# A gated recurrence over 512 steps: the rows of the input products stored first at a block's edge, and the second half's r and m transposed as they come and summed in two instructions

## The reference

```python
def step(h, x_t):
    fused = sigmoid(concatenate([x_t, h], -1) @ w_W + w_b)
    hidden_state, output_state = split(fused, 2, -1)           # r and z below
    memory_state = x_t @ wx_W + wx_b + hidden_state * (h @ wh_W + wh_b)   # m below
    h_new = output_state * h + (1.0 - output_state) * tanh(memory_state)
    return (h_new, h_new)
_, hs = lax.scan(step, h0, swapaxes(x, 0, 1))
return x + swapaxes(hs, 0, 1)
```

## Time and profile before

| | us |
|---|---|
| median of 3 runs | 1673.91 |
| lowest and highest run | 1670.84, 1674.57 |
| the profiled execution | 1674.5 |
| its span, first to last instruction | 1672.7 |
| busy: PE / PEld | 1627.8 / 1343.3 |
| busy: DVE / ACT / POOL | 1203.1 / 890.7 / 568.7 |
| share of PE in the chain that ended last | 72% |
| mean granted PE clock | 0.996 |

### The profile page before, as it was taken

The page is one execution under the profiler, slowest core; times in us unless marked ns, Lnnn a source line. Parts: engine busy times, 40 slices in busy tenths (PEclk is TensorE's granted clock), DMA queues, the critical chain, the costliest instruction groups (busy, mean ns, idle before and its releaser), DMA issues.

```text
span 1672.7 us, 211594 instructions
## 1 busy us (share of the span) xinstructions
PE 1627.8 (97%) x94336; PEld 1343.3 (80%) x94336; DVE 1203.1 (72%) x5272; ACT 890.7 (53%) x4621; POOL 568.7 (34%) x2571
## 2 busy tenths in 40 slices
PE   5999999999999999999999999999999999999998
PEld 3788888888888888888888888888888888888887
DVE  3677777777777777777777777777777777777776
ACT  2455555555555555555555555555555555555554
POOL 1233333333333333333333333333333333333333
PEclk8999999999999999999999999999999999999999
DMA  6111111111111111111111111111111111111111
GB/s 199 32 48 46 51 46 38 51 48 48 46 43 45 46 51 48 46 36 51 49 47 51 46 38 46 52 49 46 35 54 48 46 51 46 38 51 49 48 46 39
DMA packets 194889, 83.27 MB, mean 50 GB/s; under 512 B 123200, under 2 KB 194368, under 8 KB 194880
## 3 DMA queue, kind: packets, MB, share of 16 engines
q1 hardware_dynamic: 193824, 82.47, 18.3%
q10 hardware_dynamic: 1056, 0.67, 0.2%
HBM read 49.30 MB, written 33.75 MB: 50 GB/s over the span
## 4 chain that ended last, share of the span: by engine, by line
PE 72%; DMA 9%; SPq 9%; DVE 4%; issue 3%; ACT 1%; POOL 1%; ACTq 0%; POOLq 0%; DVEq 0%
PE ps L265 43%; PE ps L274 15%; PE ps L256 14%; DMA x_rows<-xs_biased 5%; SPq L197 4%; DMA ahead<-x_rows 3%; SPq L193 2%; SPq L241 1%; SPq L221 1%; DVE h L457 1%; DVE turned_rm L432 1%; DMA wx<-in_w_x 1%; ACT ps L348 1%; DVE m_pre_parts L449 1%; POOL y L549 0%
## 5 line engine op out<-in xcount | busy, mean ns | idle before, releaser
L265 PE MATMUL ps<-wh,h 128*8 128x64 f32 x65536 | 1209.2, 220 | 35.3 <-ACT ps L348 29.2
L265 PEld LDWEIGHTS ps<-wh,h 128*8 128x8 f32 x65536 | 963.2, 93 | 312.6 <-DVE h L457 290.2
L539 POOL TENSOR_TENSOR h<-h 128x16 f32<-128x16 f32 x1026 | 224.7, 219 | 1018.0 <-DVE h L457 1014.1
L274 PE MATMUL ps<-w_parts,h 128*24 128x128 bf16 x24576 | 532.8, 219 | 0.0
L274 PEld LDWEIGHTS ps<-w_parts,h 128*24 128x24 bf16 x24576 | 431.8, 121 | 0.0
L256 PE MATMUL ps<-wx,x_grp 128*32 128x384 f32 x4096 | 425.0, 486 | 0.0
L359 ACT ACTIVATE m_by<-turned_r 128x16 f32<-128x16 f32 x512 | 112.1, 219 | 541.0 <-DVE turned_r L425 541.0
L457 DVE TENSOR_TENSOR_SCAN h<-h_by,h 128x48 f32<-128x48 f32 x1024 | 259.3, 253 | 161.0 <-ACT h L372 161.0
L425 DVE STREAM_TRANSPOSE turned_r<-ps 128x64 f32<-128x64 f32 x512 | 127.8, 250 | 242.6 <-PE ps L265 229.9
L366 ACT ACTIVATE h_by<-turned_z 128x16 f32<-128x16 f32 x1024 | 227.8, 222 | 99.0 <-DVE turned_z L436 63.5
L541 POOL TENSOR_TENSOR h<-h 128x16 f32<-128x16 f32 x1026 | 224.5, 219 | 80.3
(11 more groups left out here) (30 smaller groups left out, 422.1 us busy)
## 6 DMA issues: line engine op xcount, KB each, us to landing
x_rows<-xs_biased SPq DMA_DIRECT2D x128, 192.0 KB, 1.9
ahead<-x_rows SPq DMA_DIRECT2D x512, 32.0 KB
ahead<-x_rows SPq DMA_DIRECT2D x1024, 8.0 KB
x_sb<-in_x SPq DMA_DIRECT2D x34, 256.0 KB, 3.3
x_grp<-in_x SPq DMA_DIRECT2D x516, 16.0 KB, 1.7
out_h<-y SPq DMA_DIRECT2D x32, 256.0 KB, 2.7
wx<-in_w_x SPq DMA_DIRECT2D x4, 768.0 KB, 9.1
wh<-in_w_h SPq DMA_DIRECT2D x4, 512.0 KB, 7.3
```

The lines of the kernel that those rows point to most:

```text
L265: mm = pe.matmul(ps[Q * j:Q * j + B, bank, 0:W], h_of(s - 1, k), wh[:, k, j, at:at + W], start=False, stop=(k == KC - 1), skip_group_check ...
L274: mm = pe.matmul(ps[Q * j:Q * j + PARTS * B, RM_BANK, 0:2 * W], parts_of(s - 1, k), w_parts[:, k, part, j], start=False, stop=(k == KC - 1 ...
L539: pool.tensor_tensor(mid(1, s, o), mid(0, s, o), mid_top(0, s, o), ALU.subtract).then_inc(left_once[o], 1)
```

## The change

Three things are changed. (1) SP: a block's pass begins with the first `put_ahead`; the store of the previous block's y comes behind it, then the load of x; the first pass is written out ahead of the loop, and the last store follows it. (2) DVE: `turn_rm` writes its 128 elements in the order in which they come, with no rearranging pattern. The sum of r's three parts reads them with a step of 8 elements and keeps 48 elements of input. A second reduction of the same shape does the same for m, so the scan for m of the second half has 32 elements in place of 64. Order: sum of r, scan of h (first half), sum of m, `turn_z(1)`, scan of m. The scan of m now waits for three semaphores in place of one. (3) POOL: a new instruction in each step adds zeros to m's input part to place it beside the sum. It waits for `turn_rm`, and the scan of m waits for it. Three memsets at the start change.

```diff
-        turned_rm = sb("turned_rm", [P, 2, HB, ROWS])
+        turned_rm = sb("turned_rm", [P, 2 * HC, Q])
...
-            with sp.Fori(0, BLOCKS) as i:
-                cols = bass.ds(sp.snap((i + 2) % BLOCKS * TOK), TOK)
-                sp.wait_ge(x_loaded, sp.snap(i * 16 + 16))
+            def store_y(i, which):
+                sp.wait_ge(y_added, held(sp, i * STEPS + 2 * STEPS))
+                sp.sem_inc(y_taken, 1)
+                sp.dma_start(out_flat[:, :, bass.ds(held(sp, i * TOK), TOK)],
+                             y[:, bass.ds(which, 1)].rearrange("p a c t b -> p (a c) (t b)")).then_inc(y_stored, 16)
+            def pass_of(i, before):
+                sp.wait_ge(x_biased, held(sp, i * PER_BLOCK + 2))
+                put_ahead(sp, 1, held(sp, (i * PER_BLOCK + 2) * 16))
+                if before is not None:
+                    store_y(before, held(sp, before % 2))
+                cols = bass.ds(held(sp, (i + 2) % BLOCKS * TOK), TOK)
+                sp.wait_ge(x_loaded, held(sp, i * 16 + 16))
                 sp.dma_start(x_sb[:, :, cols], x_flat[:, :, cols]).then_inc(x_loaded, 16)
-                sp.wait_ge(x_biased, sp.snap(i * PER_BLOCK + 2))
-                put_ahead(sp, 1, sp.snap((i * PER_BLOCK + 2) * 16))
                 for g in range(PER_BLOCK):
-                    turn = sp.snap(i * PER_BLOCK + (g + 1))
-                    grp_cols = bass.ds(sp.snap((i * PER_BLOCK + (g + 3)) % GROUPS * GT), GT)
+                    turn = held(sp, i * PER_BLOCK + (g + 1))
+                    grp_cols = bass.ds(held(sp, (i * PER_BLOCK + (g + 3)) % GROUPS * GT), GT)
                     for k in range(KC):
                         if k < KC - 1:
                             sp.wait_ge(x_used[k], turn)
                         else:
-                            sp.wait_ge(x_product, sp.snap(i * PER_BLOCK + (g + 3)))
+                            sp.wait_ge(x_product, held(sp, i * PER_BLOCK + (g + 3)))
                         load_x_grp(k, grp_cols)
                     if g < PER_BLOCK - 1:
-                        sp.wait_ge(x_biased, sp.snap(i * PER_BLOCK + (g + 3)))
-                        put_ahead(sp, g % SLOTS, sp.snap((i * PER_BLOCK + (g + 3)) * 16))
-                sp.wait_ge(y_added, sp.snap(i * STEPS + 2 * STEPS))
-                sp.sem_inc(y_taken, 1)
-                sp.dma_start(out_flat[:, :, bass.ds(sp.snap(i * TOK), TOK)],
-                             y[:, bass.ds(sp.snap(i % 2), 1)].rearrange("p a c t b -> p (a c) (t b)"))\
-                    .then_inc(y_stored, 16)
+                        sp.wait_ge(x_biased, held(sp, i * PER_BLOCK + (g + 3)))
+                        put_ahead(sp, g % SLOTS, held(sp, (i * PER_BLOCK + (g + 3)) * 16))
+            pass_of(0, None)
+            with sp.Fori(1, BLOCKS) as i:
+                pass_of(i, sp.snap(i - 1))
+            store_y(BLOCKS - 1, (BLOCKS - 1) % 2)
...
             def turn_rm():
-                return dve.transpose(turned_rm.rearrange("p g (c b) w -> p (g c) w b", b=B),
-                                     ps[:, RM_BANK, 0:2 * W].rearrange("p (c q) -> p c q", q=Q))
+                return dve.transpose(turned_rm[:, :, :], ps[:, RM_BANK, 0:2 * W].rearrange("p (c q) -> p c q", q=Q))
             def turn_z(o):
                 return dve.transpose(turned_z[:, o], ps[:, Z_BANK[o], 0:W].rearrange("p (c q) -> p c q", q=Q))
-            def sum_r():
-                return dve.tensor_reduce(pre_r[:, :], turned_rm[:, 0, :, 0:PARTS], AX.X, ALU.add)
-            def mix_m_first():
-                return dve.tensor_tensor_scan(m_pre[:, :, :].rearrange("p i w -> p (i w)"),
-                                              m_by[:, :, :].rearrange("p i w -> p (i w)"),
-                                              turned_m[:, 0].rearrange("p i w -> p (i w)"), 0.0, ALU.mult, ALU.add)
-            def mix_m_second():
-                return dve.tensor_tensor_scan(m_pre_parts[:, :, :].rearrange("p i w -> p (i w)"),
-                                              m_by_parts[:, :, :].rearrange("p i w -> p (i w)"),
-                                              turned_rm[:, 1].rearrange("p i w -> p (i w)"), 0.0, ALU.mult, ALU.add)
+            def sum_parts(g):
+                return dve.tensor_reduce(summed[:, g, :, 0].rearrange("p (c b) -> p c b", b=B),
+                                         turned_rm[:, HC * g:HC * (g + 1)].rearrange("p c (w b) -> p c b w", b=B)
+                                         [:, :, :, 0:PARTS], AX.X, ALU.add)
+            def mix_m(o, add):
+                return dve.tensor_tensor_scan(m_pre[:, o].rearrange("p i w -> p (i w)"),
+                                              m_by[:, o].rearrange("p i w -> p (i w)"),
+                                              add.rearrange("p i w -> p (i w)"), 0.0, ALU.mult, ALU.add)
...
-                mix_m_first().then_inc(m_pre_ready[0], 1)
+                mix_m(0, turned_m[:, 0]).then_inc(m_pre_ready[0], 1)
                 dve.wait_ge(rm_done, nxt)
                 turn_rm().then_inc(rm_turned, 1)
                 dve.wait_ge(rm_turned, nxt)
-                sum_r().then_inc(r_summed, 1)
+                sum_parts(0).then_inc(r_summed, 1)
                 mix_h(0, s, nxt)
+                sum_parts(1).then_inc(m_summed, 1)
                 dve.wait_ge(z_done[1], nxt)
                 turn_z(1).then_inc(z_turned[1], 1)
                 dve.wait_ge(r_ready[1], nxt)
-                mix_m_second().then_inc(m_pre_ready[1], 1)
+                dve.wait_ge(x_moved, nxt)
+                dve.wait_ge(m_summed, nxt)
+                mix_m(1, summed[:, 1]).then_inc(m_pre_ready[1], 1)
                 mix_h(1, s, nxt)
...
+            pool.memset(nothing[:, :, :], 0.0).then_inc(ahead_cleared, 1)
...
+                    pool.wait_ge(rm_turned, held(pool, t0 + (s + 1)))
+                    pool.tensor_tensor(summed[:, 1, :, 1].rearrange("p (c b) -> p c b", b=B),
+                                       turned_rm[:, HC:2 * HC, PARTS * B:ROWS * B], nothing[:, :, :], ALU.add)\
+                        .then_inc(x_moved, 1)
```

More of the change, by code:

```diff
@@ L89, in build @@
         turned_m = sb("turned_m", [P, ROWS // PAIR, HB, PAIR])
-        turned_rm = sb("turned_rm", [P, 2, HB, ROWS])
+        turned_rm = sb("turned_rm", [P, 2 * HC, Q])
         turned_z = sb("turned_z", [P, HALVES, HC, Q])
[L92 to L98, removed]
+        summed = sb("summed", [P, 2, HB, PAIR])
+        m_by = sb("m_by", [P, HALVES, HB, PAIR])
+        m_pre = sb("m_pre", [P, HALVES, HB, PAIR])
+        nothing = sb("nothing", [P, HC, B])
         h_by = sb("h_by", [P, HALVES, HB, TRI])
@@ L162, in build @@
         r_summed = sem("r_summed")
+        m_summed = sem("m_summed")
+        x_moved = sem("x_moved")
         x_product = sem("x_product")
@@ L358, in reset_first @@
             def reset_first():
-                act.activation(m_by[:, :, 1].rearrange("p (c b) -> p c b", b=B), turned_r[:, :, 0:B], ACT.Sigmoid)\
+                act.activation(m_by[:, 0, :, 1].rearrange("p (c b) -> p c b", b=B), turned_r[:, :, 0:B], ACT.Sigmoid)\
                     .then_inc(r_ready[0], 1)
             def reset_second():
-                act.activation(m_by_parts[:, :, PARTS], pre_r[:, :], ACT.Sigmoid).then_inc(r_ready[1], 1)
+                act.activation(m_by[:, 1, :, 1], summed[:, 0, :, 0], ACT.Sigmoid).then_inc(r_ready[1], 1)
             def update(o):
@@ L370, in new @@
                 n_twice = h[:, (s - 1) % RING, o, 1:1 + REGION].rearrange("p (b c w) -> p c b w", c=HC, w=TRI)[:, :, :, 0::2]
-                pre = (m_pre[:, :, 1], m_pre_parts[:, :, PARTS])[o].rearrange("p (c b) -> p c b", b=B)
+                pre = m_pre[:, o, :, 1].rearrange("p (c b) -> p c b", b=B)
                 act.activation(n_twice, pre.unsqueeze(3).to_broadcast([P, HC, B, 2]), ACT.Tanh)\
@@ L496, in _ @@
             dve.memset(h[:, :, :, :], 0.0).then_inc(start_h, 1)
-            dve.memset(m_by[:, :, :], 0.0).then_inc(constants, 1)
-            dve.memset(m_by_parts[:, :, :], 0.0).then_inc(constants, 1)
+            dve.memset(m_by[:, :, :, :], 0.0).then_inc(constants, 1)
             dve.memset(h_by[:, :, :, :], 0.0).then_inc(constants, 1)
+            dve.wait_ge(constants, 2)
+            dve.memset(h_by[:, :, :, 1], -1.0).then_inc(constants, 1)
             dve.wait_ge(constants, 3)
-            dve.memset(m_by_parts[:, :, 1:PARTS], 1.0).then_inc(constants, 1)
-            dve.memset(h_by[:, :, :, 1], -1.0).then_inc(constants, 1)
-            dve.wait_ge(constants, 5)
             dve.wait_ge(h0_loaded, 16)
@@ L552, in _ @@
             pool.sem_inc(y_added, STEPS)
+            pool.memset(nothing[:, :, :], 0.0).then_inc(ahead_cleared, 1)
             pool.memset(ahead[:, :, :, :], 0.0).then_inc(ahead_cleared, 1)
             pool.wait_ge(bias_h_loaded, 16)
-            pool.wait_ge(ahead_cleared, 1)
+            pool.wait_ge(ahead_cleared, 2)
             for o in range(HALVES):
```

## The result

The changed kernel takes 1634.98 us (median of 4 runs, 1634.35 to 1636.53), the one before 1673.58 us (1670.84 to 1674.57): a ratio of 0.9778, 95% interval 0.9763 to 0.9792, 38.6 us less. The profiled execution's span fell from 1672.7 to 1632.2 us.

What follows compares the result with a forecast made beforehand. DVE's chain was taken to bind at 3.14 us a step, with PE right behind it. 1674.5 - 20.5 (edges) - 14 (steps) = 1640.0 us profiled, 1639.5 as median; range 1633 to 1656.

Steps and rivals of the forecast that it cites:

- SP's new order: At block edges, issuing the copy to `x_rows` 2.7 us earlier removes ACT's wait for `ahead`: gain 20.5 us.
- The transposition: `turn_rm` on DVE gets faster with the new write pattern: -0.10 us, bounds 0 and 0.11.
- The sums: On DVE, the sum of r in another reading order: +0.04 us; the new sum of m takes 0.13 or 0.17.
- The scan of m: DVE's scan of 32 elements in place of 64: 0.20 us, ending 0.88 after the first sum starts.
- A: Loop through the first half (PE's second group, `turn_rm`, sum, scan of h, PE): 3.14 us a step, forecast 3.08.
- loop B: Loop through the second half (sum, sigmoid, scan of m, tanh, scan of h, PE): 3.14 us, forecast 3.11.
- PE's floor: PE's own work in a step: 3.10 to 3.12 us, taken as the bound at 3.11 after the change.
- POOL: POOL's new 0.22 us instruction runs in idle time beside the first half's scan of h: cost taken as 0.
- Rival 1: `turn_rm` stays at 0.42 us and the sum at 0.20, only the edges gain: 1653 us, chance 0.26.
- Rival 2: `turn_rm` stays and both DVE sums read slower, 0.07 us more a step: 1689 us, chance 0.07.
- Rival 3: POOL's instruction holds the scan of h, 0.14 us in both loops: 1710 us, or 1725 or more; chance 0.05.
- Rival 4: ACT's wait at block edges stays, as something other than SP's queue delays the rows: 1660 us, chance 0.03.

Runs made afterwards that it cites:

- before: The kernel without the change, measured beside each set of runs: 1673.58 us.
- runs 4 and 5: The changed kernel with `turn_rm`'s elements, in unchanged order, written 8 bytes apart, then 16 bytes apart: 1634.6 us and 1702.68 us.
- run 1: The kernel before with only SP's queue reordered, DVE, POOL and layouts untouched: 1655.45 us, ratio 0.9887.
- after: The kernel with the whole change: 1634.98 us, ratio 0.9778.
- run 6: The kernel after with PE's input products in the loop over 192 of 384 columns: 1613.32 us.
- run 3: The kernel after with `turn_rm` written in the old pattern, both sums and POOL's instruction reading that layout: 1668.43 us, ratio 0.9968.
- run 5: The kernel after with `turn_rm`'s elements written 16 bytes apart, order unchanged: 1702.68 us.
- run 8: The kernel after with POOL's new instruction moving 64 elements in place of 16: 1662.59 us.
- run 9: The kernel after with the sum of r over one part of three, so the first scan of h starts sooner: 1634.69 us.

## Why the prediction was right, point by point

- **SP's new order**: 20.5 us forecast, 18.6 measured alone and 20.2 in the edge steps of the trace. The mechanism was right: the copy went out 0.03 us behind the data. The rows have more time to spare than the 1.9 us forecast. The last `ahead` DMA is issued by 840.68, ACT went 1.36 behind that point where it waited for them (before), and it reads the rows at 845.03: some 3.0 us. The copy is also 1.2 us quicker without the large transfers ahead of it, which the forecast named but gave no time.
- **The transposition**: -0.10 forecast, -0.109 measured. The choice between "3 ns an element" and "a dear write" was made from the slope of additions, and runs 4 and 5 bear it out.
- **The sums**: +0.04 for the other reading order was wrong; 203 became 208 ns (page rows of run 1 and the sum of r in after). That is the term of DVE's loops that was mis-sized. `turn_z(1)` starts 0.10 behind the sum of m and not 0.17.
- **The scan of m**: starts 0.607 behind the first sum where 0.68 was said, takes 0.225 in place of 0.20, and ends at 0.83 where 0.88 was said. Its duration was taken 0.025 too short; why it isn't shorter no run tells.
- **Loops after**: A forecast 3.08, found 3.102 - 0.075 = 3.03; B forecast 3.11, found 3.05. Neither stood ahead of PE in the forecast, so the error of the sums cost nothing of the time. It hid the room, though: the forecast had loop B level with PE, and run 6 finds it 0.05 behind.
- **PE's floor**: this is most of what the forecast missed. It was put at 3.112 from rows of 10 ns, and it is 3.102; 500 x 0.010 = 5 us. The working had 3.10 to 3.12 and named the reason: the two groups of 1.02 held some 0.01 each of a start behind a wait. They take 1.01 and 1.00 in after. Run 6 shows that PE is what bounds the step there.
- **The sum**: the gain from 1674.5 was put at 34.5 us for the profiled execution and came to 40.2, 5.7 more. That the median lies only 4.5 below the forecast is chance in which executions were profiled: after's profiled one lies 0.6 below its median, before's lay 0.6 above.
- **POOL**: the scan of h is not held, as forecast, but by a hair (250 ns for 248). Its start at 80 ns meets the hold's end at 80; the rows gave no sign that the margin was that thin, and I had not worked it out.

**The rivals.** Rival 1 had its condition and its price apart. `turn_rm` at 426 ns and the sum at 203 in the changed kernel are run 3, and it takes 1668 us, not 1653: the price left out what the second sum and the new order add to loop B, 0.026 us a step or 13 us. 1655 us is run 1, which has none of the new work. So the upper end of the range, 1656, was set too low for the rival that it was to cover; as the transposition did become faster, this was not put to the test. Rival 2 (1689) has the condition of run 5, a dear write and slower sums; its step is 0.097 us above before's 3.141, not 0.07, and its one execution takes 1703. Rival 3 (POOL holds the scan) is real as a mechanism and costs nothing at this size and distance; with 64 elements it costs 28 us (run 8). The hold ends well before POOL's shown 0.22 or 0.32 us do. Rival 4 is refuted by run 1.

## What to carry to other kernels

Where two loops of engines and one engine's own work all have the same length, sum each of them from the rows before pricing an edit: a saving in one loop is worth only the distance to the next bound, here 0.039 of 0.11 us, and the rest becomes room in which new work is free. On a queue that issues DMAs, put what the next stage waits for first, and what is needed a block later behind it. If a short DVE instruction is longer than others of its size, look at the spacing of what it writes.

## What the runs showed of the hardware

- A DVE transposition of 128 fp32 elements takes 317 ns with its elements 4 or 8 bytes apart and 431 with 16, 0.9 ns more for an element. A reduction that reads 48 elements takes 203 to 208 ns when three or four of them share a line of 16 bytes, one behind the other or not, 223 when two do, and 245 when each element is in its own.
- A POOL instruction with SBUF inputs holds up a DVE scan with two SBUF inputs that starts behind it: until some 80 ns behind its start for 16 elements (after and run 9; 89 in run 3, which reads them 16 bytes apart), and 186 for 64 (run 8). The Trainium skill, SBUF — State Buffer, § Who interferes with whom, says that the later of the two is blocked until the first finishes, and that a reduction is not touched. The trace agrees that the scan is held, but the hold ended 136 ns before the shown end of POOL's 322 ns, and the shown ends of POOL are rough. That a reduction is not touched isn't tested here: the reduction of 209 ns beside the 64 elements had started 45 ns ahead of POOL, and no run has one that starts well within the hold.
- The scan of m in the kernel before met a hold too: where it started 0.05 to 0.06 behind L539 it took 304 ns in the mean, at 0.06 to 0.07 299, and at 0.07 to 0.08 292, which is also its median in the edge steps, where no POOL instruction had started in the last 0.1 us.
- A copy to `x_rows` takes 1.88 us from its issue to that of the first `ahead` DMA, which waits for its landing, and 3.08 in the mean where it was issued 0.75 us behind the load of x and 2.1 behind the store of y.
